# A second, transposed copy of x for the first graph layer's products (two-layer GNN kernel)

## What is computed

```
h = max(layernorm(x), 0);  x = x + h + elu(rgcn(t5norm(h))) @ wo      # first layer
h = max(layernorm(x), 0);  x = x + gat(h)                             # second layer

layernorm(x) = (x - mean(x)) / sqrt(var(x) + 1e-5)
t5norm(h)    = weight * h * rsqrt(mean(h*h) + 1e-6)
rgcn(n)      = n @ W_root + bias + sum over r of (mean over edges of type r of n[src] @ W_rel[r])
gat(h)       = elu(attention-weighted sum of (h @ W)[dst])
```

## The kernel before, in words

| engine | in step s, in this order |
|---|---|
| TensorE | transposed(s-1), products(s-2) |
| ScalarE | transposed(s-1), messages(s-2), normed(s+1) |
| VectorE | transposed(s-1), messages(s-2), moments(s+1) |
| GpSimd | residual(s) |
| SyncE | store_xh(s), load_x(s+2) |

## Time and profile before

### The profile page before, as it was taken

The page is one execution under the profiler, slowest core; times in us unless marked ns, Lnnn a source line. Parts: engine busy times, 40 slices in busy tenths (PEclk is TensorE's granted clock), DMA queues, the critical chain, the costliest instruction groups (busy, mean ns, idle before and its releaser), DMA issues.

```text
span 513.4 us, 7812 instructions
## 1 busy us (share of the span) xinstructions
PE 495.0 (96%) x2983; PEld 426.4 (83%) x2983; DVE 374.9 (73%) x644; ACT 226.6 (44%) x382; POOL 74.6 (15%) x72
## 2 busy tenths in 40 slices
PE   3999999999999999999999999999999999999995
PEld 2889989988988998898888888888888888888885
DVE  4846885599889999998955555557598877877623
ACT  5865443415966666668722222334133323322201
POOL 1362213100000000000000000000083333332300
PEclk9999999999999999999999999999999999999999
DMA  9972273404013235237911111000023322222211
GB/s 253 230 241 83 80 225 116 130 2 114 2 46 109 87 98 144 81 123 275 323 49 41 40 43 49 31 0 1 0 80 95 87 81 73 68 80 81 80 43 44
DMA packets 22186, 49.15 MB, mean 96 GB/s; under 512 B 4798, under 2 KB 10709, under 8 KB 22018
## 3 DMA queue, kind: packets, MB, share of 16 engines
q1 hardware_dynamic: 20879, 44.66, 29.5%
q10 hardware_dynamic: 1008, 3.67, 2.0%
q0 software_dynamic: 256, 0.26, 0.2%
HBM read 33.05 MB, written 16.85 MB: 97 GB/s over the span
## 4 chain that ended last, share of the span: by engine, by line
PE 89%; DVE 5%; ACT 3%; issue 1%; DMA 1%; ACTq 0%; SPq 0%; DVEq 0%
PE ps L1330 11%; PE ps L1595 9%; PE ps L1597 9%; PE ps L1596 9%; PE ps L1489 8%; PE ps L1577 7%; PE ps L1578 7%; PE ps L1576 7%; PE ps L1399 4%; PE ps L1548 2%; PE ps L1418 2%; PE ps L1550 2%; PE ps L1549 2%; PE ps L1562 1%; PE ps L1380 1%; PE ps L1374 1%
## 5 line engine op out<-in xcount | busy, mean ns | idle before, releaser
L1595 PE MATMUL ps<-h_hi,att_hi 125*125 125x512 f32 (+1 forms) x190 | 73.5, 387 | 0.0
L1596 PE MATMUL ps<-h_lo,att_hi 125*125 125x512 f32 (+1 forms) x190 | 72.6, 382 | 0.0
L1597 PE MATMUL ps<-h_hi,att_lo 125*125 125x512 f32 (+1 forms) x190 | 72.5, 382 | 0.0
L1576 PE MATMUL ps<-wg,gT_hi 128*125 128x512 f32 x160 | 63.7, 398 | 0.0
L1577 PE MATMUL ps<-wg,gT_hi 128*125 128x512 f32 x160 | 63.1, 394 | 0.0
L1578 PE MATMUL ps<-wg,gT_lo 128*125 128x512 f32 x160 | 63.0, 394 | 0.0
L1489 PE MATMUL ps<-msg_hi,adj_hi 125*125 125x288 f32 x180 | 50.2, 303 | 0.2 <-ACT adj_hi L596 0.2
L1489 PE MATMUL ps<-msg_lo,adj_hi 125*125 125x286 f32 x180 | 45.9, 295 | 0.0
L471 POOL TENSOR_TENSOR some<-first_att 125x625 f32<-125x625 f32 x1 | 2.4, 2440 | 276.4 <-DVE first_att L1159 276.4
L691 ACT ACTIVATE em<-ps,rinv 125x512 f32<-125x512 f32 (+1 forms) x21 | 14.0, 668 | 64.2 <-DVE hp L1203 64.2
L1597 PEld LDWEIGHTS ps<-h_hi,att_lo 125*125 125x125 f32 x190 | 35.2, 186 | 7.9
(11 more groups left out here) (215 smaller groups left out, 1116.8 us busy)
## 6 DMA issues: line engine op xcount, KB each, us to landing
xt<-in_x SPq DMA_DIRECT2D x10, 448.0 KB
xh_scratch<-xt SPq DMA_DIRECT2D x10, 448.0 KB
xt<-xh_scratch SPq DMA_DIRECT2D x10, 448.0 KB
x_scratch<-xt SPq DMA_DIRECT2D x10, 448.0 KB
x1t<-x_scratch SPq DMA_DIRECT2D x10, 448.0 KB
xr<-x_scratch SPq DMA_DIRECT2D x10, 448.0 KB
out_x<-xr SPq DMA_DIRECT2D x19, 224.0 KB
wg_raw<-in_L_gnn_W ACTq DMA_DIRECT2D x7, 512.0 KB, 7.4
```

The costliest lines, as they stand in the source:

```text
L1576: M.matmul(to, hi, wg[k][:, 0, cut], start=n == 0, stop=False)
L1595: M.matmul(to, hi[:, s, :], h_hi[:, s, cut], start=s == 0, stop=False)
L1596: M.matmul(to, hi[:, s, :], h_lo[:, s, cut], start=False, stop=False)
L1597: return M.matmul(to, lo[:, s, :], h_hi[:, s, cut], start=False, stop=s == TILES - 1)
```

## The change

The host passes a second copy of x, `x_by_column`, laid out for each tile as [128 features of a slice, 8 slices, 125 rows]. Tiles 0 and 1 are as before. For tiles 2 to 9:

- SyncE loads the tile's transposed copy into `xc` (`load_columns`), 128 partitions of 4000 bytes.
- TensorE transposes the mean column of `mv`, spread over 128 columns, once (`means_spread`), so that each partition holds the 125 means; ScalarE copies it to `means` (`means_out`).
- GpSimd subtracts the means from `xc` (`centred`).
- ScalarE writes relu(xc) to `hT_hi` (`raised`), VectorE max(xc, 0) - hT_hi to `hT_lo`. The division by the deviation is left out there, and 1/deviation is multiplied into the factor of the messages (VectorE's `mean_square`).
- `ht` is still made by ScalarE, for the residual and the sum of squares; TensorE no longer reads it.

```
 (SyncE)
+            def load_columns(t, b):
+                if t >= COLUMNS + 2:
+                    sp.wait_ge(S["hT_lo_rdy"], data(t - 2))
+                sp.dma_start(xc[b][:], x_by_column[t]).then_inc(S["xc_in"][b], 16)
...
+            load_columns(2, 0)
+            load_columns(3, 1)
             store_xh(0, 0)
             store_xh(1, 1)
             load_x(4, 0)
             load_x(5, 1)
             store_xh(2, 0)
+            load_columns(4, 0)
             store_xh(3, 1)
...
                 store_xh(t, t % 2)
                 if t + 2 < TILES:
                     load_x(t + 2, t % 2)
+                if t + 1 < TILES:
+                    load_columns(t + 1, (t + 1) % 2)
 (GpSimd)
             pool.wait_ge(S["w_split"], KT - 1)
-            for t in range(AHEAD):
-                residual(t, t % 2, t // 2)
+            def centred(t, b, d):
+                pool.wait_ge(S["means_rdy"], column(t))
+                pool.wait_ge(S["xc_in"][b], columns_in(t))
+                G.tensor_tensor(xc[b][:], xc[b][:], means[b][:].unsqueeze(1).broadcast_to([P, KT, T]), ALU.subtract).then_inc(S["cent_rdy"], 1)
+            centred(2, 0, 1)
+            residual(0, 0, 0)
+            residual(1, 1, 0)
+            centred(3, 1, 1)
+            residual(2, 0, 1)
+            residual(3, 1, 1)
             more_constants()
-            pipeline((residual, 0), steps=(AHEAD, TILES - 2))
+            residual(4, 0, 2)
+            pipeline((centred, 0), (residual, -1), steps=(AHEAD, TILES - 3))
             gather_windows()
-            pipeline((residual, 0), steps=(TILES - 2, TILES))
+            pipeline((centred, 0), (residual, -1), steps=(TILES - 3, TILES))
 (ScalarE)
             def norm(t, b):
                 act.wait_ge(S["rstd_rdy"], data(t))
-                act.wait_ge(S["hT_ps"], room(t))
+                if t < COLUMNS + 2:
+                    act.wait_ge(S["hT_ps"], data(t - 2) if t >= COLUMNS else room(t))
...
+            def means_out(t, b, d):
+                act.wait_ge(S["spread_ps"], column(t))
+                if t >= COLUMNS + 2:
+                    act.wait_ge(S["cent_rdy"], column(t - 2))
+                A.copy(means[b][:], bank(b, P, T)).then_inc(S["means_rdy"], 1)
+
+            def raised(t, b, d):
+                act.wait_ge(S["cent_rdy"], column(t))
+                act.wait_ge(S["g_ps"], room(t))
+                A.activation(hT_hi[b][:], xc[b][:], ACT.Relu).then_inc(S["hT_hi_rdy"], 1)
...
             deviation(2, 0)
+            means_out(2, 0, 1)
             norm(2, 0)
             deviation(3, 1)
+            means_out(3, 1, 1)
             norm(3, 1)
             messages(0, 0, 0)
-            transposed(2, 0, 1)
+            raised(2, 0, 1)
             mean_square(2, 0)
             mean_square(3, 1)
             normed(4, 0, 2)
             messages(1, 1, 0)
             pads()
-            pipeline((transposed, 1), (messages, 2), (normed, -1), steps=(AHEAD, TILES + 1))
+            pipeline((means_out, 0), (raised, 1), (messages, 2), (normed, -1), steps=(AHEAD, TILES + 1))
 (VectorE)
             def low_parts(t, b):
                 dve.wait_ge(S["hT_hi_rdy"], data(t))
+                if t >= COLUMNS:
+                    V.scalar_tensor_tensor(hT_lo[b][:], xc[b][:], 0.0, hT_hi[b][:].bitcast(F32), ALU.max, ALU.subtract).then_inc(S["hT_lo_rdy"], 1)
+                    return
...
+                link(V.reciprocal(stats1[:, bass.ds(t, 1), 5], stats1[:, bass.ds(t, 1), 5]))
+                V.tensor_tensor(stats1[:, bass.ds(t, 1), 5], stats1[:, bass.ds(t, 1), 5], stats1[:, bass.ds(t, 1), 2], ALU.mult).then_inc(S["rms_rdy"], 1)
 (TensorE)
+            def means_spread(t, b, d):
+                pe.wait_ge(S["var_rdy"], data(t))
+                if t < COLUMNS + 2:
+                    pe.wait_ge(S["hT_lo_rdy"], data(COLUMNS - 1))
+                else:
+                    pe.wait_ge(S["means_rdy"], column(t - 2))
+                M.transpose(bank(b, P, T), mv[b][:, 0:1].broadcast_to([T, P]), ident[0:T, 0:T]).then_inc(S["spread_ps"], 1)
...
             def stage1(first, end):
-                pipeline((transposed, 1), (products, 2), steps=(first, end))
+                pipeline((means_spread, 0), (products, 2), steps=(first, end))
...
             products_of(0, 7)
-            transposed(2, 0, 1)
+            means_spread(2, 0, 1)
+            means_spread(3, 1, 1)
             products_of(1, 7)
             stage1(AHEAD, 8)
```

More of the change, by code:

```diff
@@ L4, with rgcn_gat_kernel @@
 from contextlib import ExitStack
-def rgcn_gat_kernel(nc, x, src, dst, edge_type, ln_weight, w_rel, w_root, conv_bias, wo_weight, w_gat, a_gat, out):
+def rgcn_gat_kernel(nc, x, x_by_column, src, dst, edge_type, ln_weight, w_rel, w_root, conv_bias, wo_weight, w_gat, a_gat, out):
     F32, R32, BF16, F16 = mybir.dt.float32, mybir.dt.float32r, mybir.dt.bfloat16, mybir.dt.float16
@@ L49, in rgcn_gat_kernel @@
     AHEAD = 4
+    COLUMNS = 2
     BAND = 112
@@ L97, in came_x, with column, columns_in @@
         return came(t if t < 2 else t - 2, b)
+    def column(t):
+        return t - COLUMNS + 1
+    def columns_in(t):
+        return (t - COLUMNS) // 2 * 16 + 16
     def left(t, b):
@@ L147, in rgcn_gat_kernel @@
         first_rows_of.close()
+        columns_of = ExitStack()
+        sb(columns_of, "below_xc", [P, 8256], BF16)
+        xc = [sb(columns_of, f"xc{b}", [P, KT, T], F32) for b in range(2)]
+        columns_of.close()
         zero_adj_of = ExitStack()
@@ L191, in rgcn_gat_kernel @@
         assert end1 <= h_end and end2 <= h_end
+        (*means,), end1 = lay(end1, *pairs_of("means", [P, T], F32))
+        assert end1 <= h_end
         (msg_hi, msg_lo), at = lay(h_end, ("msg_hi", [T, TILES, RELS, FP], R32), ("msg_lo", [T, TILES, RELS, F], R32))
@@ L235, in rgcn_gat_kernel @@
         tp_bank = lambda h: ps[:, h, 0:4 * T].rearrange("p (k n) -> p k n", n=T)
-        first_tp = lambda t, h: tp_bank(6 + h if t == AHEAD - 1 else h)
+        first_tp = lambda t, h: tp_bank(h)
         heads = lambda b, h, ends: ps[0:T, 2 if h == 2 else 4 + 2 * b + h, 0:ends[1] - ends[0]]
@@ L249, in columns @@
             return adj[:, :, first:first + GW * WD].rearrange("p r (n d) -> p r n d", d=WD)
-        names = """edges_in lnw_in lnw_ps w_split h1_rdy bias_in g_ps wo_split xh_rdy x1_rdy o_ps wg_rdy a_in gT_ps h_dve
+        names = """edges_in lnw_in lnw_ps w_split h1_rdy bias_in spread_ps means_rdy cent_rdy g_ps wo_split xh_rdy x1_rdy o_ps wg_rdy a_in gT_ps h_dve
             res_rdy zeros consts more_consts sd_rdy ssq_rdy rm_rdy hT_hi_rdy g_act win_out c_used e_rdy yT_hi_rdy
@@ L259, in rgcn_gat_kernel @@
         S = {n: sem(n) for n in names}
-        for n in ("x_in", "x_ahead", "xh_out", "xh_ahead", "xb_in", "x1_in", "xr_in", "x1_out", "out_done"):
+        for n in ("x_in", "xc_in", "x_ahead", "xh_out", "xh_ahead", "xb_in", "x1_in", "xr_in", "x1_out", "out_done"):
             S[n] = [sem(f"{n}{b}") for b in range(2)]
@@ L933, in mean_square @@
                 dve.wait_ge(S["rm_rdy"], data(t))
-                V.reciprocal(stats1[:, bass.ds(t, 1), 5], stats1[:, bass.ds(t, 1), 5]).then_inc(S["rms_rdy"], 1)
+                if t < COLUMNS:
+                    V.reciprocal(stats1[:, bass.ds(t, 1), 5], stats1[:, bass.ds(t, 1), 5]).then_inc(S["rms_rdy"], 1)
+                    return
+                link(V.reciprocal(stats1[:, bass.ds(t, 1), 5], stats1[:, bass.ds(t, 1), 5]))
+                V.tensor_tensor(stats1[:, bass.ds(t, 1), 5], stats1[:, bass.ds(t, 1), 5], stats1[:, bass.ds(t, 1), 2], ALU.mult).then_inc(S["rms_rdy"], 1)
             def messages(t, b, d):
@@ L1353, in transposed @@
                 pe.wait_ge(S["h1_rdy"], data(t))
-                if t != AHEAD - 1:
-                    pe.wait_ge(S["hT_lo_rdy"], room1(t))
+                pe.wait_ge(S["hT_lo_rdy"], room1(t))
                 for k in range(KT):
@@ L1690, in _ @@
                 second_layer()
-INS = ["x", "src", "dst", "edge_type_2", "L0_gnn_ln_weight", "L0_gnn_W_rel", "L0_gnn_W_root", "L0_gnn_conv_bias",
+INS = ["x", "x_by_column", "src", "dst", "edge_type_2", "L0_gnn_ln_weight", "L0_gnn_W_rel", "L0_gnn_W_root", "L0_gnn_conv_bias",
        "L0_gnn_wo_weight", "L1_gnn_W", "L1_gnn_a"]
@@ L1701 @@
     arrays, args = {}, []
+    n_tiles, n_slices = 10, 8
+    rows, columns = inputs["x"].shape[0] // n_tiles, inputs["x"].shape[1] // n_slices
+    by_column = np.asarray(inputs["x"]).reshape(n_tiles, rows, n_slices, columns).transpose(0, 3, 2, 1)
     for name in INS:
-        a = np.ascontiguousarray(inputs[name])
+        a = np.ascontiguousarray(by_column if name == "x_by_column" else inputs[name])
         arrays[f"in_{name}"] = a
```

## The result

| | kernel before | kernel after |
|---|---|---|
| median (all runs) | 514.93 us (514.48 to 516.79) | 557.32 us (556.11 to 558.31) |
| ratio, 95% interval | 1 | 1.0815 [1.0789, 1.084] |
| profiled execution | span 513.4 us | 558.04 us, span 556.2 us |
| mean granted clock | 0.998 | 0.959 |

The change costs 42.4 us; the forecast was 28.8. The page's head against the earlier trace rows: the chain holds less of TensorE and more of VectorE, and the granted clock, in tenths, has a five, sevens and eights in the first stage, where before had nines throughout.

A forecast was written before the change was run, and what follows sets the result against it. TensorE, with 89% of the chain, was taken to bound the kernel. Opening +12.3, products(2) to the windows' transposes +17.3, tile 9's transposes -0.8: together +28.8, so 514.8 + 28.8 = 543.6 us, range 540 to 552.

The forecast's parts named there:

- The mechanism: First stage: the spread waits for var(t), behind messages(t-3) on VectorE, and holds up products(t-2); TensorE idles 3.6 us.
- The waits of the steps: TensorE at tiles 5 to 9: idles 3.6 us at each, where it idled nothing, plus 1.0 at tile 9.
- The slip of 1.0 for tile 9: GpSimd's subtraction(7) queues behind the window gather, so var(9) and tile 9's wait slip 0.5 to 1.7 us, taken as 1.0.
- The low part (7): VectorE, after the end of products(5): ends at 14.7 us, or 15.9 if it must wait for residual(8).
- The opening: Before products(2): a chain from subtraction(2) through low part (2) to spread(4) moves their start from 34.72 to 47.0, +12.3 us.
- Tile 9's transposes: TensorE behind the windows' transposes at 96.95: tile 9's transposes fall out there, -0.8 us.
- I add 2.1 once, for products(2): Cold start of TensorE after idling about 14 us in the opening: 2.1 us lost until full speed, counted once.
- the first rival: TensorE's five idle stretches of 3.6 us or more each bring a slow start, 5 x 2.1 = 10.5 us: 554 us; chance 0.20.
- nothing behind the first stage has slack to give back: After the first stage: no slack returns the loss, since VectorE's rows of windows follow at the same distance as today.

The follow-up runs named there:

- before_held: Kernel before, all transposes kept, with only a TensorE wait for the mean of tile t added at the start of step t from tile 5: 543.54 us, 1.0547 of before.
- filled: Changed kernel plus 17 matmuls on the weights, result unread, ahead of each TensorE wait for the mean from tile 5 on: 549.44 us, 1.0649 of before.
- loads_only: Kernel before plus the eight transposed 512 KB loads on SyncE's queue, their data read by nobody: 515.17 us, 1.0002 of before.
- all_low_first: Changed kernel, opening reordered, subtraction(7) ahead of the gather, VectorE's order low part, next tile's statistics, messages: 520.42 us, 1.010 of before.
- all_ordered: Changed kernel, opening reordered, next tile's statistics first in VectorE's step, subtraction(7) ahead of the gather: 522.65 us, 1.0134 of before.
- steps_ordered: Changed kernel with its opening, next tile's statistics first in VectorE's step, subtraction(7) ahead of the window gather: 533.22 us, 1.0357 of before.
- half_filled: Changed kernel plus 8 matmuls on the weights, instead of 17, ahead of each TensorE wait for the mean from tile 5: 551.16 us, 1.0688 of before.

## Why the prediction was wrong

*The mechanism: right.* The queue order puts `mv` between the end of one tile's products and the next tile's; before_held shows that this wait alone costs 28 us. The change is slower, as given.

*The waits of the steps: right in their sum, one of them by luck.* Five waits of 3.65, 3.65, 3.65, 3.30 and 4.64 are 18.9 us, against 5 x 3.6 + 1.0 = 19.0. The slip of 1.0 for tile 9 measured 4.64 - 3.65 = 1.0, and the road is the one given up to subtraction(7), which starts at 115.37, behind the gather. Behind it two errors cancel, and the 1.0 is luck:

```profile
117.48 2.40 POOL L460 TENSOR_TENSOR xt<-ht,xt 125x1024 f32<-125x1024 f32 x1
119.85 2.14 POOL L484 TENSOR_TENSOR xc<-xc,means 128x1000 f32<-128x1000 f32 x1
...
118.63 4.42 DVE L967 SCALAR_TENSOR_TENSOR hT_lo<-xc,hT_hi 128x1000 fp32r<-128x1000 f32 x1 [6.53 <-ACT hT_hi L567]
```

The low part (7) is held not by residual(8) alone, as I had allowed, but by subtraction(8) as well: it ends at 123.05, 17.4 us behind the end of products(5), where I gave 14.7 to 15.9. And the products of that step were slow, so that without the low part VectorE would have begun messages(6) at 16.7, where I gave 14.2; it began them at 17.7. At full clock (filled) tile 9 waits 7.31 us, 3.66 more than a plain wait, and the slip lies outside my 0.5 to 1.7.

*The opening: the chain right, the sum in part by luck.* +12.3 given, +13.1 measured. The subtraction took 2.13 where I took 2.35, and the low part (2) waited for the end of residual(2), as given. But that end came at 42.8, not 43.8, and the low part ended at 41.67 + 2.21 = 43.88, 1.2 us ahead of the 45.1 given. What I had not got is the last link: an instruction of 125x1 that took 2.11 us beside residual(3), to 46.10, and pushed the statistics from about 44.2 to 46.02. The one error hides most of the other.

*Tile 9's transposes: right in themselves, half of it lost again.* Products(8) start 0.35 us behind the windows' transposes (138.33 to 138.68), before 1.21 (96.95 to 98.16): 0.86 gained. Products(9) then wait 0.42 us for `hT_lo`, which they did not before. From the windows' transposes to the next stage's first product with the messages it is 25.0 us before and 24.7 after, so -0.3 in place of -0.8. The instruction prices held (`raised` 1.04, copy 0.27, spread 0.13 to the next start).

*The step that failed: "I add 2.1 once, for products(2)".* The clock term was mis-sized by its count, not by its price: 2.1 us for one slow start is near the mean of 2.2 measured, but there were six. The products of a tile, 9.6 us at full speed, took 12.2, 11.15, 12.2, 11.1, 12.1 and 12.2 us in tiles 2 to 7: 13.4 us lost, in six slow starts of 1.5 to 2.6. That is the first rival, "the clock falls in every wait", which I gave 0.20 and 554 us. I held against it that "no warm stretch of before contains such a gap, so no row shows a fall". That was no evidence: the longest gap of before in this stretch is 0.51 us, so its trace is silent on what one of 3.6 does, and the only row that has a gap of that length shows a slow start behind it. The page of the Trainium skill that the prediction named, TensorE: Matmul & The Clock Gate, HAM oscillation, describes this pattern, bursts of matmuls that begin at half clock after each wait for data; the trace agrees, six waits out of six. Weighed properly, this rival was the likeliest case.

With 13.4 in place of 2.1 and 13.1 in place of 12.3, the sum is 543.6 + 11.3 + 0.8 = 555.7. In the profiles' spans, which differ by 42.8 us, the opening has +13.1, the stretch from products(2) to the windows' transposes +28.3 (62.2 became 90.5, where I gave +17.3), the one from there to the first product with the messages -0.3, and the rest +1.8.

*The last 1.8 us: the place is known, the cause open.* From the first product with the messages to the end, before took 391.4 us and after 393.2, with the same instructions. The two keep step for 111 us; then, where the first layer passes into the second, after falls 2.0 us behind in some 30 us. TensorE waits 0.40 us for `yb` there before; after it waits 0.72 for `yb` and 0.73 for `wg`, the second layer's weights, for which it did not wait before (view of waits, after):

```profile
PE ps L1636 <- DVE wg L1151: 0.7, 1, 0.7
```

I had written that nothing behind the first stage has slack to give back; I had not allowed that something there could be lost. The stretch took 390.5 to 391.4 us in the three kernels with the first stage of before (before, before_held, loads_only), 390.9 in filled and 392.3 to 393.6 in the other eight with the change. So it may well belong to the change, but no run here says by what road.

*Where the gain went.* The transposes removed were worth 0.63 us a tile. With the waits ordered as short as I could, all_low_first is still 5.5 us above before, and in its profiled execution, 2.2 us above its median, there are 5.7 us of waits at spreads, 2.2 at products(2), two slow starts, and a full VectorE. The rows show one way in which GpSimd's second instruction a tile fills VectorE: the subtraction at 54.06 holds a `quot` instruction of 0.35 us for 2.19. That this and the low part make up the whole difference is argued; no run prices them apart.

## What to carry to other kernels

Before work is taken off the bounding engine, ask what its queue will wait for instead: here one small transpose in place of eight (0.78 us) needed a number that comes 3.6 us later, and that wait alone cost 28 us. Price every new gap in TensorE's stream twice, once for its length and once for a slow start of 1.5 to 2.6 us behind it, and do not take one row of full speed behind such a gap for safety: gaps of 2.06 to 2.20 and of 3.65 us went both ways. And moving elementwise work to GpSimd is not free for VectorE: a VectorE instruction of the kinds in these rows that starts inside one of GpSimd's does its own work when GpSimd's has ended, and at times when the next one has ended too.

## What the runs showed of the hardware

- Slow starts. Behind TensorE waits of 3.30 us or more (29 in these kernels from the wait ahead of products(2) to the windows), products at the 1.2 GHz level followed 28 times; the exception is the second 3.65 of before_held. Behind waits of 2.06 to 2.20 they followed in 4 of 7 cases, and behind the one of 2.86 too. In all_low_first they came 1.2 us after a wait of 1.77, and in all_ordered after 0.93 and 0.74 us in quick succession, a microsecond into the products, while 0.79 and 0.74 in the same succession in steps_ordered, and single waits of 1.58 (steps_ordered), 1.59 (all_low_first) and 1.67 (half_filled), had none behind them:

```profile
58.22 0.32 PE L1423 MATMUL ps<-ident,mv 125*128 125x125 f32 x1 [0.93 <-DVE mv L957]
59.28 0.46 PE L1388 MATMUL ps<-w_hi,hT_hi 128*125 128x430 f32 x1 [0.74 <-DVE hT_lo L973]
...
60.39 0.56 PE L1388 MATMUL ps<-w_hi,hT_lo 128*125 128x430 f32 x1
```

- A slow start had 7 to 9 slow products or 14 to 16 in nearly all cases (5 to 12 in before_held, where the transposes took part of it), so a price of about 1.5 us or about 2.6.
- Contention is a wait, not a slower pace, and it reaches the smallest instructions. The low part of 128x1000 took 1.20 alone, and 2.21, 2.98, 3.63 and 4.42 where it started inside a GpSimd instruction, and each time it ended 1.05 to 1.07 us behind the end of that one or of the next; 125x1 took 2.11 us beside a residual, where it takes 0.16, and ended 0.02 behind it; the `quot` instructions ended 0.21 behind. It goes the other way too: residual(3) of after, which began at 42.77 while the low part (2) was at work until 43.88, took 3.31 us and not 2.4. And it is not two-input instructions alone, for the `quot` rows above have one input in SBUF.
- Removing a slowdown can uncover another wait: in filled the clock gave back some 9 us (10.8 lost by the products of tiles 3 to 7 became some 1.6), and 2.7 of them went into tile 9's wait (7.3 for 4.64).
